# A decoder layer on one core: the end of attention written out by hand on free score banks, and the first expert's weights loaded in four column parts

## The reference, cut to what matters

```python
x = x + mamba(layernorm(x))                        # state space block, 512 channels x 16 states
x = x + cross_attention(layernorm(x), ctx, pos)    # 16 heads of 16, 77 context rows, rotary angles on q only
x = x + moe(layernorm(x))                          # 8 experts, the best 2 of each token
# moe: logits = xn @ gate_w.T; softmax; top 2, weights scaled to sum 1
#      gu = xn @ gate_up_w[e].T; h = up * gelu(gate); out += weight * (h @ down_w[e].T)
```

## Time and profile before

| | us |
|---|---|
| median of 3 runs | 2060.79 (2059.44 to 2063.51) |
| the profiled execution | 2057.14 |
| its span, first to last instruction | 2055.0 |
| TensorE matmul busy in it | 1867.7 (91%) |
| VectorE, ScalarE, GpSimd busy | 1165.8, 1101.3, 1099.4 |
| mean granted TensorE clock | 0.976 of full |

### The profile page before, as it was taken

How to read it: one execution, slowest core, us unless ns; L and a number is a source line. 1 busy time by engine, 2 the same in 40 slices (tenths; PEclk the granted TensorE clock), 3 DMA queues, 4 the chain that set the end, 5 groups by cost and what they waited for, 6 DMA issues and landing times.

```text
span 2055.0 us, 29468 instructions
## 1 busy us (share of the span) xinstructions
PE 1867.7 (91%) x10630; PEld 1519.3 (74%) x10630; DVE 1165.8 (57%) x1760; ACT 1101.3 (54%) x2157; POOL 1099.4 (53%) x806
## 2 busy tenths in 40 slices
PE   5889999989898988878999982999999999999998
PEld 2667676767676867766666651788888888888897
DVE  4899998999999998975677753111111111111111
ACT  3898989898989998935767660111111111111111
POOL 1687878777877877844658854222222322222131
PEclk8999999999999999999999995899999999999999
DMA  4121211121121114001111013944444343444441
GB/s 118 35 63 42 63 52 63 52 58 57 44 71 42 63 43 124 18 21 46 32 42 42 26 59 110 380 137 127 127 113 144 108 149 106 125 129 110 139 152 16
DMA packets 98131, 177.21 MB, mean 86 GB/s; under 512 B 24211, under 2 KB 68627, under 8 KB 87732
## 3 DMA queue, kind: packets, MB, share of 16 engines
q1 hardware_dynamic: 82308, 156.63, 22.7%
q0 software_dynamic: 15680, 18.69, 5.5%
HBM read 152.81 MB, written 22.82 MB: 85 GB/s over the span
## 4 chain that ended last, share of the span: by engine, by line
PE 49%; ACT 4%; DVE 3%; POOL 1%; issue 1%; DMA 1%; POOLq 0%; SPq 0%; DVEq 0%; ACTq 0%
PE e_ps L1643 24%; PE e_ps L1656 12%; PE m_ps L1417 3%; PE m_ps L1347 2%; PE m_ps L1392 2%; PE m_ps L1403 1%; ACT t_probs L1005 1%; PE m_ps L1340 1%; ACT m_a_ring L369 1%; PE m_ps L1333 1%; PE e_ps L1630 1%; ACT m_bxT L381 1%; PE m_ps L684 1%; POOL slots L953 1%; PE m_ps L593 1%
## 5 line engine op out<-in xcount | busy, mean ns | idle before, releaser
L324 POOL TENSOR_TENSOR m_hc_ring<-m_h_ring,m_c_bc 128x1024 f32<-128x1024 f32 x256 | 606.0, 2373 | 128.4 <-DVE m_h_ring L485 110.1
L1643 PE MATMUL e_ps<-e_xT,e_w 128*128 128x256 f32 (+1 forms) x2560 | 501.6, 357 | 0.8 <-ACT e_xT L1571 0.8
L1643 PEld LDWEIGHTS e_ps<-e_xT,e_w 128*128 128x128 f32 x2560 | 441.3, 191 | 51.5 <-issue 1.1
L1555 POOL DMA_INDIRECT out<-e_y,e_who x71 | 113.3, 1596 | 556.4 <-DVE e_y L1607 459.2
L576 PEld LDWEIGHTS m_ps<-m_ident,m_bxT 128*128 128x128 f32 x2048 | 234.9, 141 | 216.5 <-DVE m_h_ring L485 103.3
L369 ACT ACTIVATE m_a_ring<-m_delta,m_negA 128x512 f32<-128x512 f32 x512 | 366.3, 716 | 39.6 <-DVE m_h_ring L485 39.2
L576 PE MATMUL m_ps<-m_ident,m_bxT 128*128 128x128 f32 x2048 | 320.7, 280 | 67.6 <-DVE m_h_ring L485 61.7
L381 ACT ACTIVATE m_bxT<-m_uT,m_bT 128x512 f32<-128x512 f32 x512 | 364.6, 712 | 0.0
L1598 DVE TENSOR_TENSOR e_hT<-e_gact,e_ps 128x512 f32<-128x512 f32 x142 | 97.6, 687 | 459.7 <-ACT e_gact L1580 459.7
L485 DVE TENSOR_TENSOR_SCAN m_h_ring<-m_a_ring,m_carry,m_ps 128x512 f32<-128x512 f32 x256 | 317.4, 1271 | 27.6 <-ACT m_a_ring L369 13.5
L485 DVE TENSOR_TENSOR_SCAN m_h_ring<-m_a_ring,m_ps 128x512 f32<-128x512 f32 x256 | 304.3, 1210 | 35.7 <-ACT m_a_ring L369 12.4
(11 more groups left out here) (192 smaller groups left out, 2070.2 us busy)
## 6 DMA issues: line engine op xcount, KB each, us to landing
e_w<-in_gate_up_w SPq DMA_DIRECT2D x80, 1024.0 KB, 6.8
m_c_bc<-c_rows SPq DMA_DIRECT2D x32, 1024.0 KB, 5.9
e_w<-in_down_w SPq DMA_DIRECT2D x8, 1024.0 KB, 8.1
m_x_in<-in_x SPq DMA_DIRECT2D x8, 512.0 KB, 5.6
m_x_res<-in_x SPq DMA_DIRECT2D x8, 512.0 KB, 6.8
x<-m_x_res SPq DMA_DIRECT2D x8, 512.0 KB, 2.9
t_xa<-x SPq DMA_DIRECT2D x8, 512.0 KB, 4.6
out<-t_xa SPq DMA_DIRECT2D x8, 512.0 KB, 2.9
```

The costliest lines, as they stand in the source:

```text
L324: p.tensor_tensor(hc_ring[:, k % HC, :, :], h_ring[:, n % 2, e:e + 2, :], c_bc[:, n, :].unsqueeze(1).to_broadcast([P, 2, CT]), ALU.mult).t ...
L1555: nc.gpsimd.indirect_dma_start(out=out, out_offset=bass.IndirectOffsetOnAxis(ap=who[:, tile:tile + 1], axis=0), in_=y[:, s % 2, i, :], in_ ...
L1643: last = t.matmul(gu_bank(s, g, which)[:, f * wide:(f + 1) * wide], w1[s % W1_RING][:, c, lo:lo + P], xT[:, s % 2, c, 0:wide], start=(c == ...
```

## The change

**Attention.** The slots end at 64; slots 64 to 95 become one slot that calls a function drain() on each engine. C5, C6, C7 are the last three chunks, L is half 15, the last.

- Score banks are free in the tail, so the last jobs get banks of their own: half 15's output goes to bank 0, the two OUT jobs of chunk 7 to banks 1 and 5, the NT jobs of chunks 6 and 7 to banks 3 and 2, LG of chunk 7 to bank 1, RK of chunks 6 and 7 to banks 6 and 7. Semaphores late_nt, late_out and late_lg take the place of emptied.
- TensorE's order is new: the last product of half 14 stands ahead of the first turn of half 15; RK of chunk 5 and NT and LG of chunk 6 stand between the products of half 15; then both OUT jobs of chunk 7, RK of chunk 6, both NT jobs and LG of chunk 7, RK of chunk 7.
- VectorE: sums and reciprocals of score tiles 62 and 63 move into their own slots (one slot earlier). In drain the mean and root of chunk 6 are combined before the choice of chunk 5, and the choice of chunk 6 stands ahead of chunk 7's OUT additions.
- GpSimd: the rest of the scatters, in the same order.

```diff
-    FIRST, LAST = -2 * HT, TOTAL + 4 * HT
+    FIRST = -2 * HT
+    LATE_O_BANK = S_BANK
+    LATE_OUT_BANK = (S_BANK + 1, O_BANK)
+    LATE_NT_BANK = {C6: (S_BANK + 3, S_BANK + 2), C7: (S_BANK + 2, S_BANK + 3)}
+    LATE_LG_BANK = {C6: J_BANK, C7: S_BANK + 1}
+    RK_BANK = {C6: T_BANK, C7: T_BANK + 1}
...
 # act_program
+        def drain():
+            L = HALVES - 1
+            turned(L - 1, 4)
+            head_out(L - 1)
+            turned(L, 0)
+            root(rstd2, ln2, log2, C6, rstd2_ready)
+            turned(L, 1)
+            gap_root(C5)
+            normed(C6)
+            turned(L, 2)
+            norm_turned(C6, 0)
+            turned(L, 3)
+            norm_turned(C6, 1)
+            turned(L, 4)
+            head_out(L)
+            gap_root(C6)
+            root(rstd2, ln2, log2, C7, rstd2_ready)
+            normed(C7)
+            norm_turned(C7, 0)
+            norm_turned(C7, 1)
+            gap_root(C7)
...
 # dve_program
+        def drain():
+            shift(C6, nmr2, mv2, rstd2, rstd2_ready, nmr2_ready)
+            choose(C5, 2)
+            choose(C5, 3)
+            share_out(C5)
+            place(C5)
+            logits(C6)
+            for part in range(4):
+                choose(C6, part)
+            projected(C7, 0)
+            projected(C7, 1)
+            dve.wait_ge(late_out, 2)
+            measured(C7)
+            share_out(C6)
+            place(C6)
+            shift(C7, nmr2, mv2, rstd2, rstd2_ready, nmr2_ready)
+            logits(C7)
+            for part in range(4):
+                choose(C7, part)
+            share_out(C7)
+            place(C7)
+            list_steps()
...
-            if 0 <= g - 1 < TOTAL:
+            if 0 <= g - 1 < TOTAL - 2:
                 recip(g - 1)
             if 0 <= g + 1 < TOTAL:
                 maxima(g + 1)
+            if g >= TOTAL - 2:
+                recip(g)
...
 # pe_program
+        def late_nt_job(c, i):
+            pe.wait_ge(xn2_ready, TI * c + TI)
+            if c == C6:
+                pe.wait_ge(exp_done, TOTAL)
+            else:
+                pe.wait_ge(late_nt, 2 - i)
+            turned(lambda j: xn2s[:, c % 2, j, i * P:(i + 1) * P], nt_done, ps[:, LATE_NT_BANK[c][i], :])
+
+        def late_out_job(i):
+            pe.wait_ge(o_evac, HALVES)
+            projected(i, lambda m: oT[:, C7 % 2, m, :], wo_sb, out_done, ps[:, LATE_OUT_BANK[i], :])
+
+        def drain():
+            L = HALVES - 1
+            turn(L - 1, 4)
+            times_v(L - 1, 3)
+            times_v(L - 1, 4)
+            turn(L, 0)
+            turn(L, 1)
+            times_v(L, 0)
+            job("RK", C5, 0)
+            turn(L, 2)
+            times_v(L, 1)
+            late_nt_job(C6, 0)
+            turn(L, 3)
+            times_v(L, 2)
+            late_nt_job(C6, 1)
+            turn(L, 4)
+            times_v(L, 3)
+            late_lg_job(C6)
+            times_v(L, 4)
+            late_out_job(0)
+            late_out_job(1)
+            pe.wait_ge(tr_evac, UNITS * HALVES)
+            ranks(C6)
+            late_nt_job(C7, 0)
+            late_nt_job(C7, 1)
+            late_lg_job(C7)
+            ranks(C7)
```

```diff
+    def load_w1_part(sp, g):
+        e = sp.value_load(tables[0:1, 0, 0:1], min_val=0, max_val=E - 1)
+        n = F2 // 2 // W1_PARTS
+        for c in range(KD):
+            sp.dma_start(
+                w1[0][:, c, :].rearrange("p (w f) -> p w f", w=2)[:, :, g * n:(g + 1) * n],
+                gate_up_w[bass.ds(e, 1), c * P:(c + 1) * P, :].rearrange("a p (w f) -> (a p) w f", w=2)[:, :, g * n:(g + 1) * n]
+            ).then_inc(w1_part[g], 16)
...
 # keep_chunks
-        for r in range(W1_AHEAD):
-            weights.load_w1(sp, r)
+        weights.load_w1_part(sp, 0)
...
 # experts_phase, SyncE
             for s in range(STEPS):
-                if s >= W1_AHEAD:
+                if s == 0:
+                    sp.wait_ge(x_loaded[0], 16 * loads_of[0])
+                    for g in range(1, W1_PARTS):
+                        weights.load_w1_part(sp, g)
+                else:
...
 # experts_phase, TensorE
+                if s:
+                    pe.wait_ge(w1_loaded[s % W1_RING], 16 * KD * w1_loads_of[s])
+                else:
+                    pe.wait_ge(w1_part[0], 16 * KD)
...
                 for g in range(1, groups_of[s]):
+                    if s == 0:
+                        pe.wait_ge(w1_part[g], 16 * KD)
                     gate_up(s, g)
```

More of the change, by code:

```diff
@@ L955, in scatter @@
                 in_=rec[:, c * TI + i, k, :], in_offset=None).then_inc(scattered[c % 2], 16)
+        def drain():
+            normalise(TOTAL - 1)
+            for n in range(TOTAL - SCATTER_AT - C5 * HT + HT, 2 * TI):
+                scatter(C5 - 1, n)
+            for c in (C5, C6, C7):
+                for n in range(2 * TI):
+                    scatter(c, n)
         def slot(g):
+            if g == TOTAL:
+                return drain()
             c, q = g // HT, g % HT
@@ L1295, in slot @@
                 wait_emptied(dve, "OUT", c - 1, 1)
-                for i in range(TI):
-                    measure(c - 1, i, stats2, ln2)
-                spread(c - 1, stats2, mv2, rstd2, ln2)
+                measured(c - 1)
             for part in range(4):
@@ L1336, in values, with turned, projected @@
             last.then_inc(v_done, 1)
-        def turned(src, done):
+        def turned(src, done, bank=job_bank):
             for i in range(TI):
-                last = t.transpose(job_bank[:, i * P:(i + 1) * P], src(i), ident[:])
+                last = t.transpose(bank[:, i * P:(i + 1) * P], src(i), ident[:])
             last.then_inc(done, 1)
-        def projected(i, src, w, done):
+        def projected(i, src, w, done, bank=job_bank):
             for n in range(2):
@@ L1346, in projected, with logits, ranks @@
                 for m in range(KD):
-                    last = t.matmul(job_bank[:, n * DM:(n + 1) * DM], src(m)[:, tile * P:(tile + 1) * P],
+                    last = t.matmul(bank[:, n * DM:(n + 1) * DM], src(m)[:, tile * P:(tile + 1) * P],
                                     w[:, m, :], start=(m == 0), stop=(m == KD - 1))
             last.then_inc(done, 1)
+        def logits(bank):
+            for j in range(TI):
+                for m in range(KD):
+                    last = t.matmul(bank[:, j * E:(j + 1) * E], xn2T[:, m, j * P:(j + 1) * P], gw_sb[:, m, :],
+                                    start=(m == 0), stop=(m == KD - 1))
+            last.then_inc(lg_done, 1)
+        def ranks(c):
+            pe.wait_ge(chosen, c + 1)
+            bank, flat = rank_bank(c), upto[:].rearrange("p e i -> p (e i)")
+            t.matmul(bank[:, 0:E * TI], rank_w[:, 1, :], flat, start=True, stop=False)
+            t.matmul(bank[:, 0:E * TI], rank_w[:, 0, :], both[:].rearrange("p e i -> p (e i)"),
+                     start=False, stop=True)
+            t.matmul(bank[:, E * TI:E * TI + E], rank_w[:, 1, :], upto[:, :, TI - 1],
+                     start=True, stop=True).then_inc(rk_done, 1)
         def job(kind, c, i):
@@ L1370, in job @@
                 wait_emptied(pe, "NT", c, 1)
-                for j in range(TI):
-                    for m in range(KD):
-                        last = t.matmul(job_bank[:, j * E:(j + 1) * E], xn2T[:, m, j * P:(j + 1) * P], gw_sb[:, m, :],
-                                        start=(m == 0), stop=(m == KD - 1))
-                last.then_inc(lg_done, 1)
-            if kind == "RK":
-                pe.wait_ge(chosen, c + 1)
-                flat = upto[:].rearrange("p e i -> p (e i)")
-                t.matmul(job_bank[:, 0:E * TI], rank_w[:, 1, :], flat, start=True, stop=False)
-                t.matmul(job_bank[:, 0:E * TI], rank_w[:, 0, :], both[:].rearrange("p e i -> p (e i)"),
-                         start=False, stop=True)
-                t.matmul(job_bank[:, E * TI:E * TI + E], rank_w[:, 1, :], upto[:, :, TI - 1],
-                         start=True, stop=True).then_inc(rk_done, 1)
+                logits(job_bank)
+            if kind == "RK":
+                ranks(c)
         def scores(g):
@@ L1457, in expert_weights @@
     w1_loaded = [sem(f"e_w1_loaded{i}") for i in range(W1_RING)]
+    w1_part = [sem(f"e_w1_part{i}") for i in range(W1_PARTS)]
     w2_loaded = sem("e_w2_loaded")
@@ L1492, in experts_phase @@
     first_group = [sum(groups_of[:s]) for s in range(STEPS + 1)]
+    w1_loads_of = [len(range(s % W1_RING or W1_RING, s + 1, W1_RING)) for s in range(STEPS)]
     loads_of = [sum(len(tiles_of(r)) for r in range(s % X_RING, s + 1, X_RING)) for s in range(STEPS)]
```

98 lines of the change are left out of this document (75 added, 23 removed).

## The result

| | before | changed |
|---|---|---|
| median of the runs side by side, us | 2060.11 (2058.39 to 2063.51) | 2041.75 (2040.64 to 2043.96) |
| ratio to before | | 0.991 [0.9893, 0.9927] |
| the profiled execution, us | 2057.14 | 2040.64 |
| its span | 2055.0 | 2038.6 |
| mean granted TensorE clock | 0.976 | 0.979 |

Forecast were 2042.7, faster, in a range of 2037 to 2050. The kernel is 18.4 us faster by the medians and 16.4 by the two profiled spans. The profiled execution of the kernel before lay 3 us under its median, that of the changed kernel 1.1 us under.

A forecast was written before the change was run, and what follows sets the result against it. TensorE bounds the experts, so the gain is an earlier first expert matmul, behind attention's tail and DMA latencies. Tail -10.5, scatter -3.65, records -0.9, gather -3.05 sum to -18.1 us: 2042.7, range 2037 to 2050.

The forecast's parts named there:

- The three latencies: Last scatter, records and second gather before the experts: slowed by weights in flight; -3.65, -0.9 and -3.05 us.
- The scatter term: Landing of the last scatter: 3.1 us, the median, instead of 6.75, with 0.5 MB of weights ahead; -3.65 us.
- The barrier: Records ahead of the gather: SyncE's four record loads set the barrier 4.3 us behind the first; 4.4 instead of 5.3, -0.9.
- The tail: Attention's tail up to the last scatter: new order and own banks bring it from 1268.03 to 1257.55, -10.5 us.
- Case C: Rival: a hidden hand-over, likely VectorE or chunk 6's rows, sets the tail; bubble 2 to 5 us, about 2046; chance 0.12.
- That gain is nearly lost at once: Attention's tail: first turn of half 15 gains 2.1 us, but chunk 6's rows, behind chunk 5's choice, only 0.2.
- The quarters: Behind the gather (landing T): 1.65 us per quarter, step 1's weights issued by T + 7.8, no cost.
- case D: Rival: late weights; TensorE waits before step 1, at 182 GB/s for 3.5 us; 2046, chance 0.06.
- The low clock of the first group: First group of step 0: low clock, 5.88 us, unchanged, cost 0; longer than 6 us would show the forecast wrong.
- B: Rival: long DMA latencies are their own, not the weights' doing; only attention's 10.5 us gained; 2050.3, chance 0.08.
- E: Rival, slower: waits for quarters keep the clock down; a whole step at 1.2 GHz costs 21.2 us; chance 0.02.
- F: Rival, better: full clock in chunk 7's LG and neighbours, 3 us more gained; 2039.5, chance 0.06.

The follow-up runs named there:

- run 11: Changed kernel with one record load ahead of the barrier, as in run 6, and the first quarter issued behind the barrier too: 2039.13 us, ratio 0.9906.
- run 3: Changed kernel with all of step 0's weights (2 MB) ahead of the last scatters instead of a quarter: 2043.46 us, ratio 0.9919.
- run 6: Changed kernel with one record load ahead of the barrier instead of four, the other three behind it: 2037.58 us, ratio 0.9902.
- run 1: Changed kernel with the old loads, all 4 MB of steps 0 and 1 ahead of the last scatters (tail alone): 2049.1 us, ratio 0.9953.
- run 7: Changed kernel with the first down matrix (1 MB) loaded after the last OUT instead of at the last scores: 2038.93 us, ratio 0.991.
- run 9: Changed kernel with the edits of run 6 and run 8, three quarters from one table read, step 4's record load later: 2037.66 us, ratio 0.9902.
- run 4: Changed kernel with the sums of tiles 62 and 63 back in their old places: 2048.44 us, ratio 0.994.
- run 12: Run 10 with the three late quarters loaded as one then two together, and 2 useless products instead of 3 behind LG: 2034.8 us, ratio 0.9884.
- run 10: Run 9 plus 11 useless products of 128 columns between the barrier and the experts' first turn: 2036.58 us, ratio 0.9891.
- run 8: Changed kernel with useless TensorE products in attention's tail, 6 behind RK of chunk 6 and 3 behind LG of chunk 7: 2036.45 us, ratio 0.9894.
- run 2: Kernel before, attention as it was, with only the first weights loaded in quarters: 2049.26 us, ratio 0.9947.

## Why the prediction was right, and where its steps were off

**The number.** That 2042.7 met 2041.75 to a microsecond is partly luck. The terms that were forecast at -18.1 measured -14.1 in the traces, 4 us less. The medians show -18.4: of the 4.3 us between, 2.3 arose ahead of the changed code in these two traces, and the rest is that the profiled execution of the kernel before lay further under its median (3 us) than that of the changed one (1.1). Where its other executions lose those 3 us no trace shows. The order of the gains, and what each part rests on, came out as said below.

**The three latencies.** The argument that the long scatter and gather were the weights' doing, and would go with them, holds: the gather took 2.69 (forecast 2.8) and stayed at 2.7 to 2.8 in every run that had nothing in flight. The scatter term was mis-sized: -2.1 instead of -3.65. I had taken the median landing, 3.1 us, "since 0.5 MB is gone in under 2 us"; it landed in some 4.7 (an estimate: the record load's issue less 0.8, as in the kernel before). Run 11 shows the quarter itself as the cause, and run 3 that 2 MB in front cost 2.1 us more.

**The barrier.** The forecast that GpSimd would wait for the barrier, 4.3 us behind the first record load, and not for the records, was met to a tenth (1262.65 to 1266.9; the cast waits for L121). Run 6 shows the cause. What I had not seen is GpSimd's drain, which sets the barrier next.

**The tail, -8.6 instead of -10.5.** The way to chunk 6's LG came out as worked out: on the old time scale the turn at 1212.47 (forecast 1212.4), LG at 1221.7 (1221.8), the last product at 1223.4 (1223.5). Then the term of the first OUT was -5.0 instead of -5.8, for the hole, and the second's -1.0 was more than gone: the clock fell to 0.5 behind the hole, and both OUT took 5.41. Windows of the changed kernel:

```profile
1222.00:1226.00 4.00, 2.37 (x7) 1.83 (x7) 2.49 (x13) 0.60 (x1) 2.90 (x3) 0.78 0.43 129
1225.00:1227.00 2.00, 2.00 (x7) 1.55 (x6) 1.23 (x7) 0.20 (x1) 0.78 (x1) 0.50 0.03 1
```

Chunk 7's statistics start at 1229.96, on the old scale 1232.3: 2.5 behind the forecast, and of that 0.5 came back in front of NT, since I had booked 0.3 for chunk 6's slot numbers that didn't show. In executions without hole and fallen clock the tail gave 9.8 (run 1), 11.2 (run 7) and 11.3 (run 6) us, on both sides of my 10.5. So the mechanism and the sum were right for the packed order, and it is this variation that was missing. Case C had the size, 2 to 5 us, but named VectorE or chunk 6's rows; neither was late in the changed kernel. In runs 1 and 9 VectorE was, by the late start on the first OUT, for 1.3 to 1.4 us.

**The step that was wrong.** "That gain is nearly lost at once", of the moved sums, with 0.2 us left, is refuted by run 4. I had compared the end of the choice before and after, which is indeed the same, and concluded that the turn's 2.1 us didn't matter. But the new order puts the root of chunk 6, and with it the choice, behind the turn's copy on ScalarE; in that order the early turn is a condition of all that follows. Without it the tail loses 2.06 us at once, and two falls of the clock and a longer hole make it 6.2. The sum was right because I had costed the packed order with the turn where it now is.

**The quarters.** Nothing waited for weights, as forecast, but for the wrong reasons in part. SyncE took about 2.3 us a quarter (6.99 for three), not 1.65, and issued step 1's weights at T + 9.5 instead of T + 7.8. The price that I set for late weights was too high: the 182 GB/s of the earlier trace rows are the mean of a window that holds 295 GB/s in its first 3 us and nothing in its last 1.5, so they are no rate of a transfer, and case D's 2046 rests on them. The Trainium skill (DMA: Bandwidth & Descriptors, section Bandwidth) would rather have had fewer, larger transfers; in the changed kernel nothing waited for a quarter, so its trace shows no cost of the size, but run 12, which issues two DMAs fewer, had step 1's weights out 2.3 us earlier than run 10. The margin was small: with the first group 5 us earlier from the anchor, waits of 0.5 to 1.3 us appeared (runs 8, 10); 4.4 us earlier, none did (run 6).

**The low clock of the first group.** I took its 5.88 us as fixed, and named a low clock of over 6 us as a sign that the forecast is wrong. The group took 6.25 now, so that sign was met, at a price of 0.4 us. It took 5.1 to 6.7 over the runs without products ahead of it, so that this alone moves a profile by over 1 us; run 10 shows that 22 short passes ahead of it bring it to 3.69.

**Rivals.** B is refuted by the changed kernel and run 2, where the gather takes 2.7, and by run 1, where with the weights in front it takes 7.2; E did not occur, and D and F show only once TensorE is given products to fill its waits (runs 8, 10 and 12).

## What to carry to other kernels

A load that is issued "early, since the queue is free" can be the price of every small DMA on the chain: here 3.5 MB moved behind the gather gave 6.9 us by the traces (run 2). When an order is packed by hand, ask of each early step not what it gained by itself in the old order, but what now stands behind it on every engine. And in a chain of short dependent steps, a wait of TensorE can cost the clock for what comes after it as well: 2 us became 6 (run 4), and useless products in the waits gave 2.4 us back (run 8).

## What the runs showed of the hardware

- **Small indirect DMAs and bulk loads.** The last scatter landed 6.75 us behind its issue in the kernel before and 7.5 in run 1, both beside 4 MB, and 5.3 in run 6 and 4.7 in run 12, both beside 0.5 MB. SyncE's record load followed each of these landings by 0.8; taken off elsewhere, that gives estimates of 2.5 with nothing in flight (run 11), 4.7 beside 0.5 MB (the changed kernel) and 6.8 beside 2 MB (run 3). The gather takes 2.7 with nothing in flight, 3.7 beside 0.5 MB, 5.85 in the kernel before and 7.2 in run 1.
- **GpSimd's drain at the end of a block** ended some 2.7 us after the last scatter had landed in the kernel before and in run 6. In run 6 that is 2 us behind the record load, and in run 11 the drain ended 3.1 behind it; in both it set the barrier.
- **The clock.** In run 4's tail TensorE was at 1.2 GHz behind a wait of 1.9 us and again behind one of 2.9; in the changed kernel behind one of 1.6; in runs 1, 6 and 7, with 0.7 to 0.9, it stayed at 2.4 GHz in the same place. In runs 9, 10 and 12 the outcome differed with the same kernel code at that place: OUT took 5.41 in runs 10 and 12 and 3.72 in run 9, behind the same hand-over of 0.69. In run 12 the clock was also at half from about 1217 to 1220, behind a wait of 1.03 that the other traces with this order (all but run 4) have too, at 1.03 to 1.06, without a fall; LG of chunk 6 came 1.4 us later from the anchor for it. What decides between them is open.
- **The hole ahead of OUT** is open too, as is VectorE's late start in runs 1 and 9: in the changed kernel, ScalarE's copy of the last product started at 1223.14, 1.0 us after that product's end (1221.06 + 1.10), and VectorE's first step of the choice at the same time (1223.10), though its own input, LG, had ended at 1221.2.
